# Final transposes, adds and stores of the first eight batch pairs placed inside the last LSTM round

## The reference

```python
h = relu(einsum('ts,bsh->bth', adj, x @ Wg0 + bg0))
h = relu(einsum('ts,bsh->bth', adj, h @ Wg1 + bg1))
for p in range(1, 5):
    nw = T // p
    wins = h[:, :nw * p, :].reshape(B * nw, p, H)
    last = lstm_last(Wih[p-1], Whh[p-1], bih[p-1], bhh[p-1], wins)   # gates i, f, g, o; p steps
    h = h.at[:, arange(nw) * p + (p - 1), :].set(last)
return h
```

## Time and profile before

| what | value |
|---|---|
| median of three runs | 486.89 us (485.06 to 489.68) |
| the profiled execution | 488.37 us, its span 486.6 us |
| mean granted TensorE clock | 0.970 |
| TensorE matmul busy | 439.7 us, 90% of the span |
| VectorE busy | 389.3 us, 80% |
| ScalarE busy | 325.5 us, 67% |
| output stores | 16 of 256 KB, median 4.5 and 4.6 us from issue to landing |

### The profile page before, as it was taken

The page is one execution under the profiler, slowest core; times in us unless marked ns, Lnnn a source line. Parts: engine busy times, 40 slices in busy tenths (PEclk is TensorE's granted clock), DMA queues, the critical chain, the costliest instruction groups (busy, mean ns, idle before and its releaser), DMA issues.

```text
span 486.6 us, 8115 instructions
## 1 busy us (share of the span) xinstructions
PE 439.7 (90%) x2538; PEld 384.8 (79%) x2538; DVE 389.3 (80%) x1012; ACT 325.5 (67%) x630; POOL 65.9 (14%) x138
## 2 busy tenths in 40 slices
PE   0669777997999999999999999999999999999973
PEld 0447665886998888888887888899999988888863
DVE  2699598999676777878767788887887879889884
ACT  0676748998658787777766766776677666576530
POOL 4633895040312000000000000000000000000000
PEclk9989788999899999999999999999999999999987
DMA  8900000000000000000000000000000000000029
GB/s 244 337 3 2 1 1 0 3 0 0 2 1 0 2 0 0 0 0 0 0 2 0 1 0 2 0 2 0 1 0 1 3 0 1 0 0 2 0 84 262
DMA packets 13994, 11.67 MB, mean 24 GB/s; under 512 B 902, under 2 KB 12172, under 8 KB 13708
## 3 DMA queue, kind: packets, MB, share of 16 engines
q1 hardware_dynamic: 8176, 8.39, 5.7%
q10 hardware_dynamic: 5788, 2.91, 2.2%
HBM read 7.10 MB, written 4.19 MB: 23 GB/s over the span
## 4 chain that ended last, share of the span: by engine, by line
PE 76%; DVE 12%; ACT 5%; issue 2%; POOL 2%; DMA 1%; DVEq 0%; ACTq 0%; POOLq 0%
PE ps L931 47%; PE ps L1030 11%; PE ps L1034 6%; PE ps L911 4%; DVE score L627 2%; DVE score L668 2%; ACT v_norm L434 2%; PE ps L892 2%; PE ps L1049 2%; PE ps L896 1%; PE ps L974 1%; PE ps L923 1%; DVE stats L580 1%; DVE ebias L647 1%; POOL scale L361 1%
## 5 line engine op out<-in xcount | busy, mean ns | idle before, releaser
L536 ACT ACTIVATE work<-ps,bl 128x512 f32<-128x512 f32 (+2 forms) x204 | 111.2, 628 | 23.8 <-PE ps L1034 17.1
L931 PE MATMUL ps<-h_hi,wl_hi 128*128 128x512 f32 (+3 forms) x252 | 92.9, 369 | 1.4 <-DVE h_lo L732 1.4
L931 PE MATMUL ps<-h_hi,wl_lo 128*128 128x512 f32 (+3 forms) x252 | 92.8, 368 | 0.0
L931 PE MATMUL ps<-h_lo,wl_hi 128*128 128x512 f32 (+3 forms) x252 | 92.6, 367 | 0.0
L526 ACT ACTIVATE work<-work 128x512 f32<-128x512 f32 (+2 forms) x56 | 31.5, 571 | 45.7 <-DVE work L816 34.8
L434 ACT ACTIVATE v_norm<-xs,shift,scale 128x128 f32 (+1 forms) x128 | 52.4, 483 | 2.9 <-POOL shift L364 2.8
L931 PEld LDWEIGHTS ps<-h_hi,wl_hi 128*128 128x128 f32 x252 | 47.5, 188 | 7.7 <-DVE h_lo L732 1.6
L931 PEld LDWEIGHTS ps<-h_lo,wl_hi 128*128 128x128 f32 x252 | 47.4, 188 | 6.5
L931 PEld LDWEIGHTS ps<-h_hi,wl_lo 128*128 128x128 f32 x252 | 47.5, 188 | 5.8
L1030 PE MATMUL ps<-s_hi,wl_hi 128*128 128x512 f32 (+2 forms) x144 | 51.1, 357 | 0.0
L1030 PE MATMUL ps<-s_hi,wl_lo 128*128 128x512 f32 (+2 forms) x144 | 51.1, 357 | 0.0
(11 more groups left out here) (125 smaller groups left out, 968.9 us busy)
## 6 DMA issues: line engine op xcount, KB each, us to landing
result<-xs SPq DMA_DIRECT2D x8, 256.0 KB, 4.5
result<-xs ACTq DMA_DIRECT2D x8, 256.0 KB, 4.6
xs<-in_x SPq DMA_DIRECT2D x2, 512.0 KB, 5.2
work<-in_w_ih_t SPq DMA_DIRECT2D x1, 1024.0 KB, 10.8
work<-in_w_hh_t SPq DMA_DIRECT2D x1, 1024.0 KB, 9.1
adj_raw<-in_adj ACTq DMA_DIRECT2D x1, 256.0 KB, 8.8
adjT_raw<-in_adj_t ACTq DMA_DIRECT2D x1, 256.0 KB, 10.1
wg_raw<-in_w_gcn ACTq DMA_DIRECT2D x2, 64.0 KB
```

The lines of the kernel that those rows point to most:

```text
L536: nc.scalar.activation(lw[:, par, g, 0:cols], ps[:, 4 * par + g, 0:cols], ACT.Tanh if g == G else ACT.Sigmoid, bias=bl[:, (p - 1) * GATES ...
L931: ins = nc.tensor.matmul(dst, a, b, start=start and n_ == 0, stop=stop and n_ == 2)
```

## The change

In round 9 (`END`) each of the eight half steps now also carries the four transposes of one pair, q = 2 * k + par, so pairs 0 to 7, whose results round 8 has made. They go into banks that are free for a part of the step: pairs 0 and 1 into the F banks, which step 0 doesn't use, pair q from 2 on into the I bank of the other parity, after ScalarE has read it. TensorE may write such a bank again only after VectorE's add of that pair: gate F of step 1 waits for the adds of pairs 0 and 1, and gate I from half step (1, 1) on waits for the add of the pair before.

VectorE makes the add of pair 0 before `result_h` of the round before, that of pair 1 after the cell of (0, 1), that of pair 2 behind the `part_lo` of (0, 1), and those of pairs 3 to 7 each after the cell and the join of a half step, before `part_hi`. SyncE stores each pair as it is added.

In the last half step, (3, 1), TensorE completes gates I and G first, then F, then O, where before the high part ran over all four gates and then the low part. VectorE makes the last cell sum at once, ahead of the join, and the last `result_h` ahead of all eight remaining adds. Pairs 8 to 11 are transposed into the four banks of parity 0 (in the order G, F, O, I), 12 to 15 into those of parity 1. The last four pairs are stored in two halves of 128 KB, one from SyncE and one from ScalarE; all others by SyncE alone.

```diff
+        END = len(ROUNDS) - 1
+        WITHIN = PAIRS // 2
+        HALVED = 4
+        def bank_out(q):
+            if q < WITHIN:
+                k, par = divmod(q, 2)
+                return 4 * par + F if k == 0 else 4 * (1 - par) + I
+            return [G, F, O, I][q - WITHIN] if q < WITHIN + 4 else q - WITHIN
...
-            with sp.Fori(0, PAIRS // 2) as q:
-                sp.wait_ge(d_out, q * 2 + 1)
-                sp.dma_start(out_v[:, bass.ds(q * 8, 4), :], xs[:, bass.ds(q * 8, 4), :]).then_inc(stored, 16)
-            sp.wait_ge(stored, 16 * PAIRS)
+            for q in range(PAIRS - HALVED):
+                sp.wait_ge(d_out, q + 1)
+                sp.dma_start(out_v[:, q * 4:q * 4 + 4, :], xs[:, q * 4:q * 4 + 4, :]).then_inc(stored, 16)
+            for q in range(PAIRS - HALVED, PAIRS):
+                sp.wait_ge(d_out, q + 1)
+                sp.dma_start(out_v[:, q * 4:q * 4 + 2, :], xs[:, q * 4:q * 4 + 2, :]).then_inc(stored, 16)
+            sp.wait_ge(stored, 16 * (PAIRS + HALVED))
...
-            with act.Fori(0, PAIRS // 2) as q:
-                act.wait_ge(d_out, q * 2 + 2)
-                act.dma_start(out_v[:, bass.ds(q * 8 + 4, 4), :], xs[:, bass.ds(q * 8 + 4, 4), :]).then_inc(stored, 16)
+            for q in range(PAIRS - HALVED, PAIRS):
+                act.wait_ge(d_out, q + 1)
+                act.dma_start(out_v[:, q * 4 + 2:q * 4 + 4, :], xs[:, q * 4 + 2:q * 4 + 4, :]).then_inc(stored, 16)
...
-                if (k, par) != (steps_of(r) - 1, 1):
+                if (k, par) != (steps_of(r) - 1, 1) or r == END:
                     cell_sum(r, k, par)
...
+            def add_pair(q):
+                dve.wait_ge(d_T, q + 1)
+                xq = xs[:, q * 4:q * 4 + 4, :].rearrange("p k f -> p (k f)")
+                nc.vector.tensor_tensor(xq, ps[:, bank_out(q), :], xq, ALU.add).then_inc(d_out, 1)
...
                 full_h(r, 0, 0)
+                if r == END:
+                    add_pair(0)
                 if q == LAST:
                     result_h(r - 1, 1)
...
                             join(r, k - 1, par)
+                        if r == END and (k, par) == (0, 1):
+                            add_pair(1)
+                        elif r == END and (k, par) != (LAST - 1, 1):
+                            add_pair(2 * k + par + 1)
                         if (k, par) == (LAST - 1, 0):
                             result_h(r, par)
                         elif (k, par) != (p - 1, 1):
                             part_hi(r, k, par)
                             full_h(r, k, par)
                             part_lo(r, k, par)
+                        if r == END and (k, par) == (0, 1):
+                            add_pair(2)
+
+            result_h(END, 1)
+            for q in range(WITHIN, PAIRS):
+                add_pair(q)
...
+                            if r == END and (k, g) == (1, F):
+                                pe.wait_ge(d_out, par + 1)
+                            if r == END and g == I and 2 * k + par > 2:
+                                pe.wait_ge(d_out, 2 * k + par)
...
+                        if r == END:
+                            q = 2 * k + par
+                            if q in (0, 4):
+                                pe.wait_ge(c_h[q // 4], h_base[r])
+                            if k > 0:
+                                pe.wait_ge(c_act[1 - par], acts_before(r, k - 1 + par) + 1)
+                            transpose_pair(q)
                         if k > 0:
                             pe.wait_ge(c_hi[par], part_base[r] + k)
...
+                            for some in ([[I, G], [F], [O]] if (r, k, par) == (END, LAST - 1, 1) else [gates]):
+                                for g in some:
+                                    for part in weights(p, 1, g):
+                                        nc.tensor.matmul(ps[:, 4 * par + g, 0:cols], part, s_hi[:, par, 0:cols],
+                                                         start=False, stop=False)
+                                pe.wait_ge(c_lo[par], part_base[r] + k)
+                                for g in some:
+                                    nc.tensor.matmul(ps[:, 4 * par + g, 0:cols], weights(p, 1, g)[0],
+                                                     s_lo[:, par, 0:cols], start=False, stop=True
+                                                     ).then_inc(c_gate[par], 1)
...
+            for q in range(WITHIN, PAIRS):
+                if q == WITHIN:
                     pe.wait_ge(c_act[0], a_total - 1)
-                if q == 8:
                     pe.wait_ge(c_h[0], h_total)
-                if q == 12:
+                if q == WITHIN + 3:
+                    pe.wait_ge(d_out, WITHIN)
+                if q == WITHIN + 4:
                     pe.wait_ge(c_h[1], h_total)
...
+                transpose_pair(q)
```

More of the change, by code:

```diff
@@ L995, in weights, with transpose_pair @@
                 return wl(0, p, m)[:, c], wl(1, p, m)[:, c]
+            def transpose_pair(q):
+                for k in range(4):
+                    c = (4 * (q % 4) + k) * P
+                    ins = nc.tensor.transpose(ps[:, bank_out(q), k * P:(k + 1) * P], result_of[q // 4][:, c:c + P],
+                                              ident[:, :])
+                ins.then_inc(d_T, 1)
             for r in range(len(ROUNDS)):
@@ L1051, in _ @@
-                ins.then_inc(d_T, 1)
+                transpose_pair(q)
 def kernel(x, adj, L0_gnn_W, L0_gnn_a, L1_gnn_Wg0, L1_gnn_bg0, L1_gnn_Wg1, L1_gnn_bg1, L1_gnn_Wih, L1_gnn_Whh,
```

## The result

Over 20 runs of each kernel the median is 483.50 us after the change (481.26 to 487.40) and 488.19 us before (484.76 to 490.29). The ratio is 0.9925, with a 95% interval from 0.990 to 0.995: about 3.7 us faster (2.4 to 4.9). (The two medians differ by 4.7 us, at the upper end of this interval.) The forecast was 2.4 us faster and a time of 484.5 us, in a range of 482.0 to 487.6; right in direction, and low by 1.3 us in size. The forecast time stood on the 486.89 us of the first three runs; from the 488.19 us measured here the same 2.4 us would have led to 485.8 us, also within the range. That the time itself came out within 1.0 us of 484.5 is in part luck.

What follows compares the result with a forecast made beforehand. TensorE bounds the last LSTM round, and the stores end last behind it. Bytes -7.3, their start loss -0.2 and first add +5.1 gave -2.4 us, from the 486.89 us median to 484.5 us, range 482.0 to 487.6.

Steps and rivals of the forecast that it cites:

- Steps 1 and 2: Last round: 32 transposes cost TensorE 3.5 us; VectorE's adds fit free into half steps of 5.88 us.
- Step 3: Start of the last round: TensorE waits for adds before rewriting borrowed banks; costs 1.4 us (0.75 to 1.9).
- Step 4: Last half step: gate I complete 0.91 us earlier, cell sum ahead of the join; ScalarE's first gate at 468.71.
- Step 5: Tail: first of eight remaining adds 5.09 us later, at 473.81; TensorE no longer paces them; worth nothing in itself.
- Step 6: Stores: eight leave free during the round; the tail's 2.10 MB take 7.28 us at 288 GB/s; span 484.2 against 486.6.
- A: Rival at the round's start and first store: wait only 0.75 us, start loss vanishes; gain 3.3 us, 483.6; chance 0.15.
- B: Rival: TensorE's clock falls in the round, at its two early waits; slower, 487.8 us; chance 0.08.
- C: Rival in the tail: halved 128 KB stores run only at 230 GB/s; end 0.9 us later, 485.4; chance 0.07.
- D: Rival: nothing moves; the lengthened round (4.9 us) plus slower adds beside TensorE's writes eat all; chance 0.12.

Runs made afterwards that it cites:

- the second measurement: The changed kernel measured once more, unedited: ratio 0.9972 (0.9936 to 1.0008) to the kernel before.
- the kernel with both edits: Changed kernel with new gate orders in (1,0) and (1,1), and adds of pairs 8 to 10 ahead of the last h: ratio 0.9906 to the kernel before.

## Why the prediction was right

Times from the last round's first matmul (428.48 before, 430.20 after), forecast and seen:

| step | forecast | seen |
|---|---|---|
| 1, 2: a half step | 5.88 us | 5.92 (adds at 452.11, 458.01, 463.93, 469.85) |
| 3: add of pair 2 starts | 11.27 | 11.25 |
| 3: TensorE's first load of (1,1) | 12.00 | 12.05 |
| load behind the last LSTM load, moved by | 4.9 | 5.1 (36.49 to 41.59) |
| 4: ScalarE's first gate of (3,1) | 40.23 | 40.42 |
| 5: first of the last eight adds | 45.33 | 45.52 |
| 6: last packet | 54.7 | 54.5 |
| end | 55.7 | 55.4 |

Steps 1 and 2: a half step grew by 0.48 us (5.44 to 5.92) where 4 x 0.109 = 0.44 was taken. Doubling the transposes added 0.42 us a pair, 0.105 each, so some 0.06 us of the 0.48 is paid once a pair, however many transposes it has. The Trainium skill's 81 ns for a sustained matmul of 128 columns ("TensorE: Matmul & The Clock Gate", Back-to-back issue gap) gives, as an estimate, 0.32 us a pair; the measured 0.42 and 0.48 decide for the trace's figure. The half steps, each some 0.04 us longer than worked out, are most of the 0.2 us by which the last LSTM load came late. The adds were free from (2,0) on: no wait of TensorE for one stands in the trace there. Step 3: the waits were 0.35 and 1.14 us where 0.3 and 1.1 were worked out, and taking them away gave 1.3 us back: the cost of 1.4 is shown, not only argued. Step 4: the gate order was worth 0.9 us in one direction and 0.8 in the other, the earlier sum 0.5. Step 5: TensorE's clock stayed at the full 2.4 GHz through the last transposes, which is luck of this execution, but step 5 didn't need it. In the run with the stores held back the granted clock was 0.50 from 474.5 us and the same 16 loads took 3.27 us instead of 1.73, and the eight adds still followed each other in 4.86 us. Step 6: the end follows the stores' bytes: pushing eight stores back cost 7.5 us where 7.3 was worked out. The closing after the last packet was 0.87 us where 1.03 was taken over from before; that, and a stream that lost nearly nothing at its start (7.33 us where 7.48 were taken), is the 0.3 us by which the stretch was better. One reading was loose: the last add before the change starts 5.9 us ahead of the last packet (479.7 to 485.6), not five, which changes nothing.

The rivals: A (the waits cost less) fell with their measured length; B (the clock falls in the round) did not happen, the granted clock being 1.00 from 430.2 to 448.3 us, where the two waits lie, and from 448.3 to 471.8 us; C fell with the whole stores; D with the 5.92 us.

```profile
448.30:471.80 23.50, 23.50 (x113) 19.42 (x113) 20.95 (x41) 12.96 (x23) 0.00 (x0) 1.00 0.13 38
```

What the sum could not give is the rest of the measured 3.7 us. The last round's stretch doesn't hold it, and ahead of that round both kernels do the same work, at scattered times: over 14 profiled executions the first matmul of that round came between 424.42 and 430.20 us. From the first LSTM matmul to that one the time is fixed, 283.4 to 283.5 us in all fourteen: 145.02 to 428.48 before, 146.81 to 430.20 after, 141.05 to 424.48 in the kernel with its gates together. So the scatter arises ahead of it, in stage A and the start of stage B. The granted clock differs there, and goes with it in part. Three executions have 0.95, and they are the first to get there (140.96 to 141.05 us); but among those with 0.92, before and after included, the first LSTM matmul comes anywhere from 142.85 to 146.81 us. What else moves it is not shown. After the change, and with the gates together:

```profile
14.70:140.00 125.30, 104.88 (x663) 87.76 (x663) 106.63 (x450) 89.34 (x189) 53.27 (x102) 0.92 0.08 28
```

```profile
14.70:140.00 125.30, 108.58 (x705) 90.60 (x706) 107.75 (x459) 92.94 (x197) 53.97 (x103) 0.95 0.08 28
```

Whether the changed program shifts the odds of that scatter stays open: the second measurement (0.9972) and that of the kernel with whole stores, whose stretch is the same (0.9952), speak against it, but the intervals overlap.

## What to carry to other kernels

When output stores fill the DMA engines at the end, count bytes: the time is the first late store plus all bytes behind it, and only bytes sent off earlier, or an earlier first store with an unbroken supply, bring anything. Work moved into a full engine's stretch costs its full price there (here 5.1 us, waits included, of 7.5 gained), so look for the waits that its borrowed buffers create; writing the borrowed bank last in the next step took 1.3 us of them away for nothing. By the rule that fits the last runs, an add pulled ahead helps only until the next one that was pushed back becomes the latest.

## What was not expected of the hardware

GpSimd beside VectorE, both with two fp32 operands in SBUF: a group of three VectorE instructions that otherwise takes 1.11 us took 1.94 us while GpSimd's group of 2.88 us ran.

And TensorE's granted clock in the tail did not follow the length of the idle stretch ahead of the last transposes. Their 16 loads took 1.73 us, with the clock at 1.00, after 2.26 us of idle in the changed kernel and after 3.16 us in the kernel with its gates together. After 2.25 us of idle they took 3.04 us in the kernel without the two waits, and after 2.26 us 3.27 us in the one with its stores held back; there the clock had fallen to 0.50 by 472 and by 474.5 us. After 4.17 us of idle, with the same tail, they took 2.50 us in one kernel and 3.28 us in the other, the clock being 1.00 and 0.50 in their first microsecond. What decides it is not shown.

The weight-load rows below are of the changed kernel and of the one with only the adds moved; that of the kernel with both edits stands further up. The two stretches are of the latter two kernels.

```profile
475.94 1.73 PEld L1019 LDWEIGHTS ps<-ident,result 128*128 128x128 f32 x16 [2.26 <-DVE result L810]
```

```profile
472.77 2.50 PEld L1031 LDWEIGHTS ps<-ident,result 128*128 128x128 f32 x16 [4.17 <-DVE result L810]
```

```profile
472.50:473.50 1.00, 0.73 (x7) 0.73 (x8) 0.77 (x3) 0.00 (x0) 0.00 (x0) 1.00 0.76 229
```

```profile
472.50:473.50 1.00, 0.79 (x4) 0.80 (x5) 0.67 (x2) 0.00 (x0) 0.00 (x0) 0.50 0.82 246
```
